# A four-layer attention kernel: low-rank weights of its recurrent layer padded to full tiles, and VectorE's first scans moved up

## The reference

```
xa = ln(x);  sx = (xa of the step before) - xa
xxx = tanh((xa + sx*maa_x) @ maa_w1)            # 256 -> 5 groups of 32: low rank
xm  = xa + sx*(maa_stack + xxx @ maa_w2)        # five mixes: k, w, v, r, g
w   = exp(-exp(time_decay + tanh(xw @ td_w1) @ td_w2))    # td_w1: 256 x 64, td_w2: 64 x 256
r, k, v, g = xr@Wr.T, xk@Wk.T, xv@Wv.T, silu(xg@Wg.T)
for t:  a = k_t v_t^T;  out_t = r_t (u*a + s);  s = a + w_t * s      # 32 heads of 8 x 8
x1 = x + (groupnorm(out) * g) @ Wo.T
x2 = x1 + sigmoid(xr2@Wfr.T) * (square(relu(xk2@Wfk.T)) @ Wfv.T)     # channel mix on ln(x1)
```

## Time and profile before

| | us |
|---|---|
| three runs: median (lowest to highest) | 987.27 (984.85 to 987.67) |
| profiled execution: its span; the page gives no other time of it | 982.8 |
| PE (TensorE matmul) busy | 944.6 (96%) |
| DVE (VectorE) busy | 592.1 (60%) |
| ACT (ScalarE) busy | 462.5 (47%) |
| POOL (GpSimd) busy | 411.8 (42%) |
| 831.0 to 982.8: the recurrent layer from the first scan on | 151.8 |

### The profile page before, as it was taken

How to read it: one execution, slowest core, us unless ns; L and a number is a source line. 1 busy time by engine, 2 the same in 40 slices (tenths; PEclk the granted TensorE clock), 3 DMA queues, 4 the chain that set the end, 5 groups by cost and what they waited for, 6 DMA issues and landing times.

```text
span 982.8 us, 21494 instructions
## 1 busy us (share of the span) xinstructions
PE 944.6 (96%) x8321; PEld 795.7 (81%) x8321; DVE 592.1 (60%) x974; ACT 462.5 (47%) x1026; POOL 411.8 (42%) x572
## 2 busy tenths in 40 slices
PE   6999999989999999999999999999999999999998
PEld 4777777966788888988897888998888888678776
DVE  5899986767544433344356433344426766999883
ACT  4677874237643333333334333333342434576565
POOL 2143346875365333333246343342422862344231
PEclk9999999999999999999999999999999999999999
DMA  9100000310011110111101110111100100000000
GB/s 298 37 23 2 2 2 22 116 54 2 1 55 50 54 50 25 37 54 48 54 7 55 50 54 21 42 49 48 54 22 18 41 14 1 1 2 6 13 6 23
DMA packets 24147, 37.15 MB, mean 38 GB/s; under 512 B 4432, under 2 KB 16528, under 8 KB 23824
## 3 DMA queue, kind: packets, MB, share of 16 engines
q1 hardware_dynamic: 24080, 36.23, 11.9%
HBM read 35.17 MB, written 1.05 MB: 37 GB/s over the span
## 4 chain that ended last, share of the span: by engine, by line
PE 74%; DVE 12%; ACT 5%; issue 4%; POOL 4%; DMA 0%; DVEq 0%; ACTq 0%; POOLq 0%
PE ps L1292 18%; PE ps L790 13%; PE ps L1309 9%; PE ps L1351 6%; PE ps L1948 5%; PE ps L890 4%; PE ps L1327 4%; PE ps L1337 2%; DVE sb L2476 2%; DVE sb L656 1%; PE ps L270 1%; DVE sb L650 1%; PE ps L2026 1%; PE ps L421 1%; PE ps L2112 1%
## 5 line engine op out<-in xcount | busy, mean ns | idle before, releaser
L837 POOL TENSOR_TENSOR sb<-sb 128x256 fp32r<-128x256 f32 (+1 forms) x128 | 102.5, 801 | 278.0 <-DMA sb<-in_heads_a 144.9
L1292 PE MATMUL ps<-sb 128*128 128x512 f32 x768 | 187.7, 396 | 1.0 <-issue 1.0
L1292 PEld LDWEIGHTS ps<-sb 128*128 128x128 f32 x768 | 139.5, 188 | 33.0 <-ACT sb L1425 3.1
L790 PE MATMUL ps<-sb 128*128 128x256 f32 x1152 | 148.4, 286 | 0.0
L790 PEld LDWEIGHTS ps<-sb 128*128 128x128 f32 x1152 | 141.4, 191 | 2.1 <-issue 0.2
L839 POOL TENSOR_TENSOR sb<-sb 128x256 fp32r<-128x256 f32 (+1 forms) x128 | 115.8, 905 | 10.0
L1522 DVE SCALAR_TENSOR_TENSOR sb<-ps,sb 128x512 fp32r<-128x512 f32 x64 | 45.1, 747 | 95.6 <-ACT sb L1458 95.5
L1309 PE MATMUL ps<-sb 128*128 128x256 f32 x768 | 99.2, 285 | 0.4 <-DVE sb L1490 0.4
L1502 DVE TENSOR_REDUCE sb<-ps 128x8 f32<-128x520 f32 x32 | 22.4, 700 | 126.6 <-PE ps L1327 126.6
L1309 PEld LDWEIGHTS ps<-sb 128*128 128x128 f32 x768 | 95.0, 191 | 3.0 <-issue 0.9
L1425 ACT ACTIVATE sb<-ps,sb 128x512 f32<-128x512 f32 x64 | 43.8, 685 | 107.9 <-PE ps L1292 107.8
(11 more groups left out here) (221 smaller groups left out, 1668.2 us busy)
## 6 DMA issues: line engine op xcount, KB each, us to landing
sb<-in_heads_a SPq DMA_DIRECT2D x32, 386.0 KB, 3.0
sb<-in_heads_c SPq DMA_DIRECT2D x16, 256.0 KB, 3.6
sb<-in_heads_b SPq DMA_DIRECT2D x32, 128.0 KB, 3.1
sb<-in_mlp_a SPq DMA_DIRECT2D x16, 128.5 KB, 2.1
sb<-in_mlp_b SPq DMA_DIRECT2D x16, 128.0 KB, 2.1
sb<-in_w_r SPq DMA_DIRECT2D x1, 2048.0 KB, 7.5
sb<-in_encT SPq DMA_DIRECT2D x1, 1024.0 KB, 6.2
sb<-in_ctx SPq DMA_DIRECT2D x1, 1024.0 KB, 8.1
```

Source lines behind the costliest of these rows:

```text
L790: last = pe.matmul(m.acc(t), lhsT[x], rhs[w], start=opens and n == 0, stop=False, skip_group_check=True)
L837: pool.tensor_tensor(high, src, one, ALU.mult).then_inc(*G.did(name + "_high", u))
L1292: last = pe.matmul(m.ps[u][:, c, :], m.w_parts[u][w][:, (KD * q + k) * P:(KD * q + k + 1) * P], rows[x][:, k, c * 512:(c + 1) * 512], star ...
```

## The change

Three edits in the recurrent layer.

1. Padding. `maa_w1` gets a sixth, empty group of 64 columns, so that `lora` is three products groups of 128 output rows; `td_w1` (64 columns), `td_w2` (64 rows) and the tile `m.td` between them are padded with zeros to 128. The number of instructions stays as it was. The padded parts of the weights are loaded with them.
2. `scan0` stands in front of `products1` and `group_sum` on VectorE, right behind `mix2`, in the loop and after it.
3. `scan0` waits for `av0` alone and `scan1` for `av1` alone, instead of both for both.

```diff
-NX = 5 * 64
+NX = 6 * 64
@@ rwkv_tensor, lora
-        for n, width in enumerate((P, P, 2 * DM)):
-            cols = slice(n * P, n * P + width)
-            last = product(m.mx_ps[0:width, n * P:(n + 1) * P],
-                           [(m.maa_w1[:, k, cols], m.xl[i % 2][:, k, :]) for k in range(KD)])
+        for n in range(NX // P):
+            cols = slice(n * P, (n + 1) * P)
+            last = product(m.mx_ps[:, cols], [(m.maa_w1[:, k, cols], m.xl[i % 2][:, k, :]) for k in range(KD)])
@@ rwkv_tensor, decay1
-        product(m.td_ps[0:DD, 0:P], [(m.td_w1[:, k, :], mixed(i, MIX_W, k)) for k in range(KD)])\
+        product(m.td_ps[:, 0:P], [(m.td_w1[:, k, :], mixed(i, MIX_W, k)) for k in range(KD)])\
@@ rwkv_scalar, decay1
-        act.activation(m.td[:, :], m.td_ps[0:DD, 0:P], ACT.Tanh).then_inc(*done["td"].did(i))
+        act.activation(m.td[:, :], m.td_ps[:, 0:P], ACT.Tanh).then_inc(*done["td"].did(i))
@@ rwkv_vector, scan
-        vec.wait_ge(*done["av0"].at(i))
-        vec.wait_ge(*done["av1"].at(i))
+        vec.wait_ge(*done[f"av{part}"].at(i))
@@ rwkv_vector, the loop
+        scan0(slot - 5)
         products1(slot - 5)
         group_sum(slot - 6)
         shift(slot - 3)
         lora_rows(slot - 3)
         if slot == 3:
             mlp_split(vec, ph, m, 1, 1, 3)
-        scan0(slot - 5)
         group_rstd(slot - 6)
@@ rwkv_vector, behind the loop
+    scan0(LAST)
     products1(LAST)
     group_sum(LAST - 1)
-    scan0(LAST)
@@ build
-        m.td_w2 = m.mask_mul["cross"][0:DD, TILES * HS * 4:TILES * HS * 4 + D]
+        m.td_w2 = m.mask_mul["cross"][:, TILES * HS * 4:TILES * HS * 4 + D]
-        m.td_w1 = sb([P, KD, DD])
+        m.td_w1 = sb([P, KD, P])
-        m.td, m.og, ... = cut(1, at, [P], DD), cut(1, at, [D]), ...
+        m.td, m.og, ... = cut(1, at, [P]), cut(1, at, [D]), ...
```

More of the change, by code:

```diff
@@ L2820, in build @@
         at = [rest]
-        m.td, m.og, m.sq, m.tok, m.yT = cut(1, at, [P], DD), cut(1, at, [D]), cut(1, at, [D]), cut(1, at, [D]), cut(1, at, [KD, P])
+        m.td, m.og, m.sq, m.tok, m.yT = cut(1, at, [P]), cut(1, at, [D]), cut(1, at, [D]), cut(1, at, [D]), cut(1, at, [KD, P])
         m.xc = cut(1, at, [KD, 2, S + 1])
@@ L3050, in lay_out @@
     turned = n % 16 == p // HS
-    w1 = np.zeros((KD, P, ND, 2 * DM), np.float32)
-    w1[:, :, :, 0:DM] = L3("maa_w1").reshape(KD, P, ND, DM)
+    w1 = np.zeros((KD, P, NX // (2 * DM), 2 * DM), np.float32)
+    w1[:, :, 0:ND, 0:DM] = L3("maa_w1").reshape(KD, P, ND, DM)
     w2 = np.zeros((2, 2 * DM, 3, D), np.float32)
@@ L3071, in lay_out @@
         "w1x1": np.ascontiguousarray(np.stack([L1(n) for n in ("Wn", "Wm", "Wl", "Wo")]).transpose(2, 0, 1)),
-        "maa_w2": w2.reshape(P, 3, D), "maa_w1": w1.reshape(KD, P, NX).transpose(1, 0, 2), "td_w1": block(L3("td_w1")), "td_w2": L3("td_w2"),
+        "maa_w2": w2.reshape(P, 3, D), "maa_w1": w1.reshape(KD, P, NX).transpose(1, 0, 2), "td_w1": np.pad(block(L3("td_w1")), ((0, 0), (0, 0), (0, P - DD))),
+        "td_w2": np.pad(L3("td_w2"), ((0, P - DD), (0, 0))),
         "w_r": np.ascontiguousarray(np.stack(stack).transpose(2, 0, 1).reshape(KD, P, 8, D).transpose(1, 2, 0, 3)),
```

## The result

| us | before | after |
|---|---|---|
| first comparison: median (runs; lowest to highest) | 987.18 (4; 984.85 to 987.67) | 991.10 (4; 989.63 to 993.35) |
| second comparison, more runs | 984.15 (27; 982.48 to 988.28) | 990.18 (6; 988.60 to 993.13) |
| profiled execution, span | 982.8 | 987.8 |
| start of the last record of `mixes(0)` to the end of the span | 168.36 | 175.23 |

The kernel after is slower: the ratio is 1.0056 [1.0037, 1.0074] in the first comparison and 1.0065 [1.0043, 1.0086] in the second, which is 3.9 and 6.0 us between the medians. The forecast was +5.9 on 987.3.

What follows compares the result with a forecast made beforehand. VectorE was taken to bound the early tiles, with TensorE waiting for `products1`, and TensorE from about 883 us. 987.3 + 2.9 (queues) + 3.0 (clock) = 993.2 us, range 985.5 to 997.

Steps and rivals of the forecast that it cites:

- Tile 0, the late w: At tile 0's moved `scan0`, VectorE stalls 1.4 us for w from ScalarE, so `project(1)` starts 3.2 us later.
- `project(2)` at +4.2, `project(3)` at +5.5, `project(4)` at +4.9: Delays in us of these `project` starts, from `scan0` put ahead of `products1`, for which `project` waits.
- Tile 2, the period from `project(3)`: Period of 19.9 us before, where TensorE becomes the bound: loses 0.6 of waits (`gated`, `gate`) and 0.2 by padding.
- The padding: Fewer array mode switches save TensorE 0.63 us a tile, 1.9 over three periods, plus 0.4 before the first scan.
- The second regime: From about 883 us TensorE bounds; of 2.9 us spare before `project`, 0.9 remain, so the move costs nothing.
- The tail: Last tile: five scans gain at most 2.2 us, later `products1` costs up to 1.75; taken as +0.3.
- The queues in all: Sum of delays, padding and last tile without clock effects: +4.9 - 0.4 - 1.9 + 0.3 = +2.9 us.
- The clock: TensorE's three longer idle gaps were to cause two half-clock drops of 1.5 us each, +3.0; bounds 0 and +5.1.
- The base: Starting time 987.3 us, the median of the runs; with the profiled span 982.8, 4.5 lie around it or between executions.
- Rival A: Same loop delays, but TensorE's clock holds: 990.2 us, chance 0.21.
- Rival B: Waits mostly absorbed, the early loss about equal to the 2.3 us from padding: 987.3 us, chance 0.12.
- Rival C: VectorE stays the early bound; ended GpSimd collisions shorten two to three periods by 1.2 to 2 us: 981.0, chance 0.17.

Runs made afterwards that it cites:

- experiment 3: Kernel after with 12, 8 and 11 more filler matmuls ahead of `project(1)`, `project(2)` and `project(3)`; 989.51 us, ratio 1.0044 to before.
- experiment 4: Kernel after with `products1` in front of `scan0`, which still precedes `group_sum`, `shift` and `lora_rows`; 986.54 us, ratio 1.0014 to before.

## Why the prediction was right, step by step

- **Tile 0, the late w: right.** I had a stall of 1.4 and `project(1)` at +3.2; the stall is 1.30 and `project(1)` at +3.00 (+3.14 over the padding alone). The move in tile 0 alone costs 2.42 of queue time, so the step is shown and not only seen beside the loss.
- **`project(2)` at +4.2, `project(3)` at +5.5, `project(4)` at +4.9: right in kind, the last one low.** With the clock held (experiment 3) they are at +3.01 + 1.04 = 4.05, then 5.62, and 5.19 where my sum gives 4.8 (4.9 less the 0.13 of the padding that lies in the stretch). The period from `project(2)` was to be 18.0 and is 18.29. The gaps were to be 3.1, 2.1 and 2.6, and are 3.03, 2.14 and 2.88.
- **Tile 2, the period from `project(3)`: wrong in its terms.** I took 0.6 off for waits that go and 0.2 for the padding (which from +5.5 gives +4.7 and not the 4.9 that I wrote). The period went from 19.90 to 19.47. The padding takes its 0.62 off in full, and the waits add 0.2 where I had them fall by 0.6: that for `gated` shrank from 0.56 to 0.22, but a new one of 0.54 came, that of `mixes` (L1986, before L1987) for ScalarE's `lora` (L2211). TensorE's timeline of before, and then of the kernel with the clock held:

```profile
869.40 1.71 PE L1948 MATMUL ps<-sb 128*128 128x256 f32 x8 [0.56 <-POOL sb L2664]
871.04 1.60 PE L1987 MATMUL ps<-sb 64*128 64x128 f32 x20
```

```profile
875.11 1.57 PE L1948 MATMUL ps<-sb 128*128 128x256 f32 x8 [0.22 <-POOL sb L2662]
877.22 1.60 PE L1986 MATMUL ps<-sb 64*128 64x128 f32 x20 [0.54 <-ACT sb L2211]
```

- **The padding: right, a little less.** 0.62 a tile against 0.63, but periods of 18.14, 18.14 and 17.97 against 18.76, 18.75 and 18.38 give 1.65 over three tiles, not 1.9. The third one gains only 0.42, which is 0.14 + 0.15 + 0.14 without the 0.19 of `decay2`: no `turn` is left for this slot, so `decay2` stands right behind `gather` with its 32 output rows, and its piece of the chain is 0.64 in before (932.72) and still 0.64 with the padding alone (929.07). The 0.4 of the first tiles is all there: `project(1)` comes 0.13 earlier with the padding alone, and the way from `lora(0)` to `mixes(0)`, which lies ahead of the stretch, takes 4.21 instead of 4.52. The larger loads cost nothing that the runs show. The Trainium skill's rule on a load's time (TensorE: Matmul & The Clock Gate, section LDWEIGHTS (loading the stationary operand)) speaks of the load record alone. Here the padded loads run beside the matmuls, and the pieces of 128 columns have the pitch that they had.
- **The second regime: right.** `products1` ends at 905.15 + 1.18 = 906.3 and `project` starts at 907.30, so 1.0 of slack is left where I had 0.9. The three tiles lose nothing to the move, as the tiles 3 to 6 by themselves show.
- **The tail: +0.3, as forecast.** The two sides were not taken apart. The last tile's five scans gave 1.1 (3.51 instead of 4.65), half of the bound of 2.2, and the tail still grew by 0.32. With tile 7 in the old order (tile 0 alone, tiles 3 to 6) it didn't grow, so the 0.32 are those of tile 7's own move.
- **The queues in all: too low by 0.7.** They cost +3.90 in the stretch, which is +3.6 with the 0.3 of padding ahead of it, against 2.9. Of the difference 0.4 lies in tile 2's period and the ones before it and 0.25 in the padding of the last periods.
- **The clock: two drops of 1.5 predicted, two of 1.37 and 1.64 found**, behind the second and third gap and not behind the first. Holding the clock with filler gives 2.97 back. That it was two is luck in part: the move alone had two as well, but at other gaps, the first and the third, and tile 0 alone had one at its only gap.
- **The base: wrong.** I read 987.3 - 982.8 = 4.5 us as lying around the span. The later runs list time and span of each execution, and 1.8 lies around it (989.63 - 987.8). The profiled execution of before, 982.8 long, belongs by that to a run of 984.6, beside the fastest of the first four (984.85) and not to their median. Before has a median of 984.95 and 984.15 over 29 and 27 runs; the 987.3 of three was at the high end. The forecast of 993.2 lies 2.1 above the 991.1 measured, and its difference to before, +5.9, agrees with the +6.0 of the second comparison and not with the 3.9 of the first, whose four runs of before were high. By the profiles the queues' +3.6 and the clock's +3.0 make +6.6.
- **Rival A** (the clock holds) is what experiment 3 made of the kernel: its layer is 2.97 shorter than that of after. **Rival B** (absorbed) is refuted by the starts of `project`. **Rival C** had its premise right. The collisions end, and the rule of the Trainium skill's page SBUF — State Buffer, section SBUF: two separate sides, by which a VectorE instruction with two inputs in SBUF waits until a GpSimd instruction that reads SBUF and started first has ended, agrees with this trace: `products1`, with one operand in PSUM, takes 1.18 beside GpSimd, and `shift`, with both in SBUF, 0.82 to 1.95 instead of 0.41. Its conclusion was wrong, because `project` waits for `products1` and so for everything that is put in front of it. In part the collision has moved to `shift` (1.15 in tile 0's slot, 0.82 to 0.85 in the others of after).

## What to carry to other kernels

In a pipeline written out by hand, look first at who waits on another engine for the step that an edit pushes back. Three scans of 0.58 us ahead of `products1`, and the 1.3 us that they wait for their own input, cost 6.0 us over four tiles (0, 1, 2 and 7), while the VectorE time that they saved was worth nothing. When spans differ from run to run ahead of the change, compare from a fixed step to the end, and part the edit by tile: halves that add up show that no share is missing. Empty columns that keep TensorE in one array mode cost nothing here, where their load runs beside a matmul, and they gain only where no other change of mode stands at the same place.

## What the runs showed of the hardware

- A gap on TensorE can cost more than its length. Behind gaps of 2.1 to 3.0 us the granted clock fell to 0.51 for 3.4 us, and a `project` that fell into it took 4.90 to 5.16 us instead of 3.53, so 1.4 to 1.6 more. It didn't fall behind every such gap: after had three gaps and two drops, in each of its two profiles, and the move alone had gaps of 3.03, 1.95 and 2.70 with drops at the first and the third. Behind gaps of 0.9 to 1.4 (the padding alone, experiment 4) no drop was seen in the layer.
- In the one profile with 12, 8 and 11 more filler products in these gaps (12 take 4.38 - 1.66 = 2.7 us) the clock stayed at 1.00 through the layer.
- Each change of array mode that the padding removed had cost 0.14 to 0.19 us, and the larger tile cost nothing for its empty half.
- GpSimd's multiplication over 768 elements a partition holds up VectorE's operations with two inputs in SBUF: `shift`, started 0.14 us after it, took 1.95 us instead of 0.41, and in experiment 4 and in after it ended 0.28 us behind the end of the multiplication in every slot in which it had started beside it, early or late. A product with one operand in PSUM kept its 1.18, and `group_sum`, which has a single input, in SBUF, kept its 0.41 (848.09 in after, with the multiplication running from 847.15 to 848.96).
